# Attention with two heads per group of 32 rows, and the exponentials of ScalarE moved among its copies

## What is computed

```python
x = x + xattn(layernorm(x), ctx, ...)          # x, ctx: (16, 128, 256)
x = x + ffn(layernorm(x), ...)

def xattn(query, key, ...):                     # 16 heads of 16 numbers
    q, k, v = query @ Wq.T + bq, key @ Wk.T + bk, key @ Wv.T + bv
    att = q @ k.T / sqrt(16)                    # per head, 128 x 128
    att = where(pad_mask == 0, -1e9, att); att = where(subsq_mask == 0, -1e9, att)
    return softmax(att) @ v

def ffn(x):                                     # 12 experts, two per row, and a shared one
    logits = (x @ Wr + br) / 1.5
    top_val, top_idx = top_k(logits, 2); w = softmax(top_val)
    return shared(x) + sum(w_e * expert_e(x))   # each: GEGLU between two products
```

## Time and profile before

| | us |
|---|---|
| median of 3 runs | 661.57 (658.15 to 663.26) |
| span of the profiled execution | 661.7 |
| TensorE busy | 601.9 (91%) |
| VectorE busy | 460.1 (70%) |
| ScalarE busy | 302.4 (46%) |
| GpSimd busy | 348.7 (53%) |
| the chain that ended last, by engine | TensorE 68%, VectorE 11%, issue 7%, ScalarE 6% |

### The profile page before, as it was taken

One profiled execution on the slowest core, in us unless ns is written; L12 is line 12 of the kernel. 1 busy time (PEld: TensorE's weight loads), 2 busy tenths in 40 slices (PEclk: granted clock), 3 DMA queues, 4 the chain that ended last, 5 costly groups with the idle time before them and its releaser, 6 DMA issues.

```text
span 661.7 us, 14825 instructions
## 1 busy us (share of the span) xinstructions
PE 601.9 (91%) x4406; PEld 508.4 (77%) x4407; DVE 460.1 (70%) x1037; ACT 302.4 (46%) x677; POOL 348.7 (53%) x403
## 2 busy tenths in 40 slices
PE   7899999998887876989999999999999999997893
PEld 6677878887767765778878888788887888787792
DVE  7888888979865547766666667666776666653575
ACT  4467676655654223434444444344443444432331
POOL 3891100110294673998884893888893860006361
PEclk9999999989987977989999999999999999999798
DMA  8957465248404323345643544445633311003242
GB/s 278 333 212 258 153 223 206 88 183 295 176 28 172 122 94 86 144 156 196 223 145 109 184 170 137 139 136 209 219 137 127 125 42 40 24 18 99 77 137 79
DMA packets 47910, 98.95 MB, mean 150 GB/s; under 512 B 4736, under 2 KB 23808, under 8 KB 47872
## 3 DMA queue, kind: packets, MB, share of 16 engines
q1 hardware_dynamic: 36192, 50.40, 21.5%
q0 software_dynamic: 10976, 47.72, 21.5%
q10 hardware_dynamic: 704, 0.33, 0.2%
HBM read 57.15 MB, written 39.19 MB: 146 GB/s over the span
## 4 chain that ended last, share of the span: by engine, by line
PE 68%; DVE 11%; issue 7%; ACT 6%; another core or an unknown queue 4%; POOL 3%; DMA 1%; DVEq 0%; ACTq 0%; SPq 0%; POOLq 0%
PE ps_s L801 27%; PE ps_o L834 9%; PE ps_o L835 5%; PE ps_s L763 5%; PE ps_t L586 3%; PE ps_t L811 3%; PE ps_t L515 2%; PE ps_x L515 2%; ACT prob L1006 1%; DVE nmax L1351 1%; PE ps_s L811 1%; PE ps_o L596 1%; PE ps_x L822 1%; PE ps_s L574 1%
## 5 line engine op out<-in xcount | busy, mean ns | idle before, releaser
L801 PE MATMUL ps_s<-ring,xTh 128*128 (+1 forms) x516 | 152.2, 417 | 1.4 <-DVE xTl L1674 1.4
L1850 POOL TENSOR_TENSOR ring<-stage,ring 128x512 fp32r<-128x512 f32 x80 | 100.6, 1290 | 1.2
L801 PEld LDWEIGHTS ps_s<-ring,xTh 128*128 128x128 f32 x516 | 88.5, 189 | 16.1 <-DVE xTl L1674 1.6
L834 PE MATMUL ps_o<-ring,hTh 128*128 x258 | 97.0, 413 | 2.2 <-DVE hTl L1669 2.2
L1660 DVE TENSOR_TENSOR ag<-ps_s,up_bias 128x512 f32<-128x512 f32 x129 | 88.8, 689 | 12.4 <-PE ps_s L801 10.0
L801 PE MATMUL ps_s<-ring,xTl 128*128 (+1 forms) x258 | 80.6, 393 | 0.0
L835 PE MATMUL ps_o<-ring,hTl 128*128 x258 | 72.8, 282 | 0.0
L1836 POOL TENSOR_TENSOR ve<-mv,eps 128x2 f32<-128x2 f32 x16 | 3.9, 246 | 130.6 <-DVE mv L1390 117.2
L2036 POOL DMA_INDIRECT gath<-rows_out,idx_out x32 | 30.9, 967 | 77.2 <-DMA rows_out<-y_row 57.0
L1130 ACT ACTIVATE ps_s<-ag 128x256 f32<-128x256 f32 x129 | 50.2, 389 | 39.0 <-DVE ag L1660 37.9
L1665 DVE TENSOR_TENSOR ag<-ag,ps_s 128x256 f32<-128x256 f32 x129 | 54.3, 421 | 16.1 <-ACT ps_s L1130 0.5
(11 more groups left out here) (272 smaller groups left out, 1350.7 us busy)
## 6 DMA issues: line engine op xcount, KB each, us to landing
rows_in<-y_row SPq DMA_DIRECT2D x8, 3328.0 KB, 12.2
stage<-in_w POOLq DMA_DIRECT2D x12, 1536.0 KB
stage<-in_w POOLq DMA_DIRECT2D x12, 768.0 KB, 5.4
up_bias<-in_bias POOLq DMA_DIRECT2D x12, 768.0 KB, 4.6
xrow<-rows_in SPq DMA_DIRECT2D x43, 128.0 KB, 2.1
rows_out<-y_row SPq DMA_DIRECT2D x43, 128.0 KB, 1.7
cbuf<-in_ctx SPq DMA_DIRECT2D x8, 256.0 KB, 2.9
xn_all<-xn2p SPq DMA_DIRECT2D x8, 256.0 KB
```

The lines of the kernel that those rows point to most:

```text
L801: last = pe_.matmul(ps_s[:, i, :], x[:, c, :], weights(place, off + c * 2 * HR + i * 2 * D, 2 * D), start=n == 0, stop=n == 5)
L834: pe_.matmul(ps_o[:, :], hTh[i][:, c, :], weights(place, a, 2 * D), start=i == 0 and c == 0, stop=False)
L1850: last = pool.tensor_tensor(lo_ap[:, c:c + PIECE], src[:, c:c + PIECE], hi_ap[:, c:c + PIECE].bitcast(f32), ALU.subtract)
```

## The change

- **Two heads in a group of 32 rows.** The host orders the columns of wq and wk so that a group of 32 rows holds two heads. q and k are projected once, 256 columns in all: steps `k` and `q` of two parts take the place of `k0 k1 q0 q1`. So that a product over 32 rows gives one head's scores and not the sum of two, k is stored twice (`km_hi`, `km_lo`), once with the odd head's rows set to zero and once with the even head's; GpSimd writes these (`spread_keys`). `scores` has 24 products of 32 rows by 256 columns.
- **The context comes transposed from the host.** Step `cT` is gone; GpSimd splits the loaded context into high and low (`split_ctx`).
- **GpSimd applies both normalisations** (`normalise_x`, `normalise_rows`); VectorE's next statistics wait until it has.
- **SyncE's rounds**: load the context, then wait for the rows, save them, fill.
- **The shared expert's weights** are converted in slices inside the pairs 1 to 4, where the first loads of expert weights are issued too.
- **The order in the bodies.** A group of `values` follows each copy instead of four behind the fourth; ScalarE's exponentials stand between the second and third copies of the batch before (and between the third and the fourth of the next), ahead of its copies of k and q; `r` and `l` stand behind the last transposes.
- **Masks** come from one instruction, and the identity is scaled by the fill value.

The diff, cut:

```diff
@@ SyncE
+            sp.wait_ge(c_split, 1)
             load_ctx(1)
...
-            def pair(p, par, first, last):
-                if first:
-                    sp.wait_ge(xb_ready, index_of("cT", p, first, last) + 1)
-                    load_ctx(2)
-                else:
-                    save_xn2(p - 1)
-                sp.wait_ge(xb_ready, index_of("cT", p, first, last, first) + 1)
-                load_ctx(p + 3)
-                fill(p + 1)
+            def pair(p, first):
+
+                sp.wait_ge(c_split, p + 2)
+                load_ctx(p + 2)
+                if not first:
+                    save_xn2(p - 1)
+                fill(p + 1)
@@ TensorE, scores
-                for g in range(4):
-                    for k in (k_hi, k_lo):
+                for r in range(2):
+                    for n, (q, k) in enumerate(((q_hi, km_hi), (q_lo, km_hi), (q_hi, km_lo))):
                         for j in range(4):
...
+                            last = pe_.matmul(ps_s[:, j, r * 256:(r + 1) * 256].rearrange("p (a t) -> p a t", a=2),
+                                              q[par][rows, r, b * P:(b + 1) * P], k[par][rows, b, r, :, :],
+                                              start=False, stop=r == 1 and n == 2)
@@ TensorE, pair (not first)
                     prob_transposes(prev, 0)
+                    put("k", (0,))
                     prob_transposes(prev, 1)
+                    values(1, 1 - par, prev, (0,))
+                    put("k", (1,))
                     prob_transposes(prev, 2)
+                    values(1, 1 - par, prev, (1,))
+                    put("q", (0,))
                     prob_transposes(prev, 3)
+                    values(1, 1 - par, prev, (2,))
+                    put("q", (1,))
+                    values(1, 1 - par, prev, (3,))
+                    scores(p, par, 1)
+                    out_transposes(prev)
                     put("n")
...
+                prob_transposes(cur, 0)
+                put("v", (0,))
+                prob_transposes(cur, 1)
+                values(0, par, cur, (0,))
+                put("v", (1,))
+                prob_transposes(cur, 2)
+                values(0, par, cur, (1,))
+                put("xT", again=first)
+                prob_transposes(cur, 3)
+                values(0, par, cur, (2,))
+                put("r")
+                values(0, par, cur, (3,))
+                put("l")
+                out_transposes(cur)
+                next_scores()
@@ ScalarE, pair (not first)
                     prob_copy(prev, 0)
                     prob_copy(prev, 1)
-                    put("k0")
+                    exp(p * 4, 0)
                     prob_copy(prev, 2)
+                    sc.wait_ge(k_spread, p + 1)
+                    put("k")
                     prob_copy(prev, 3)
-                    put("k1")
                     out_copy(prev)
-                    exp(p * 4, 0)
                     exp(p * 4 + 1, 1)
-                    put("q0")
+                    put("q")
...
+                prob_copy(cur, 0)
+                prob_copy(cur, 1)
                 put("v")
+                prob_copy(cur, 2)
+                put("xT", first)
+                exp(p * 4 + 2, 2)
+                prob_copy(cur, 3)
+                put("r")
+                out_copy(cur)
                 exp(p * 4 + 3, 3)
@@ VectorE, ln1_stats and pair (not first)
+                if not (isinstance(pp, int) and pp == 0):
+                    ve.wait_ge(xn1_ready, pp)
...
                     softmax_add(p * 4, 0)
+                    softmax_shift(p * 4 + 1, 1, p * 2)
+                    put("k")
+                    if isinstance(p, int) and p == PAIRS - 3:
+                        choose(0, 0)
+                    elif not isinstance(p, int):
+                        ln1_stats(p + 3)
+                    softmax_max(p * 4 + 2, 2, p * 2 + 1)
+                    norm(p - 1, 1)
+                    put("q")
+                softmax_add(p * 4 + 2, 2)
                 if not first:
                     residual(p - 1, 1)
...
+                softmax_shift(p * 4 + 3, 3, p * 2 + 1)
+                put("xT", first)
                 norm(p, 0)
                 residual(p, 0)
@@ GpSimd
+            def split_ctx(q):
+
+                gp.wait_ge(ctx_in, 16 * (q + 1))
...
+                pool.tensor_scalar(hi[:, :, :], c_raw[:, :, :], 1.0, 0.0, ALU.mult, ALU.add).then_inc(c_hi, 1)
+                gp.wait_ge(c_hi, q + 1)
+                pool.tensor_tensor(lo[:, :, :], c_raw[:, :, :], hi[:, :, :].bitcast(f32), ALU.subtract).then_inc(c_split, 1)
...
+            for p in range(1, PAIRS - 1):
+                if p + 2 < PAIRS:
+                    split_ctx(p + 2)
+                    normalise_x(p + 2)
+                spread_keys(p + 1)
+                if p == 1:
+                    shared_up_hi()
+                if p == 2:
+                    shared_up_lo(0, W1S // 2)
+                if p == 3:
+                    shared_up_lo(W1S // 2, W1S)
+                if p == 4:
+                    shared_down()
+                    gp.wait_ge(converted, 1)
+                    load_raw1(0)
+                    load_raw2(0)
+                normalise_rows(p - 1)
```

More of the change, by code:

```diff
@@ L290, in build @@
     combined, stored = sem("combined"), sem("stored")
[L295 to L309, removed]
+    HI = ["k", "q", "xT"]
+    FIRST = ["k", "xT", "q", "v"]
+    HI_FIRST = [s for s in FIRST if s in HI]
+    first_bank = [ps_x[:, :], ps_s[:, 0, :], ps_s[:, 1, :], ps_t[:, 1, :]]
+    MASK_A = 2
     BATCHES = ((0, 8), (8, 12), (12, 16))
@@ L495, in transposes, with step @@
                 return last
-            def step(s, pp, idx, bank, first=False, parts=(0, 1)):
+            def step(s, pp, par, idx, bank, first=False, parts=(0, 1)):
                 if not first and 0 in parts:
@@ L595, in values @@
+            def values(b, par, batch, groups=(0, 1, 2, 3)):
+                for g in groups:
+                    pe.wait_ge(pt_copied, batch * 4 + g + 1)
+                    if g == 0 and not (isinstance(batch, int) and batch == 0):
+                        pe.wait_ge(normed, batch)
                     for j in range(4):
                         last = pe_.matmul(ps_o[32 * j:32 * j + VW, g * P:(g + 1) * P], v_sb[par][:, b, 4 * g + j, :],
-                                          probT[:, j, g, :], start=True, stop=True)
@@ L679, in put @@
                         return
-                    idx, bank = index_of(s, p, first, last, again), bank_of(s, p, par, first, last, again)
+                    idx, bank = index_of(s, p, first, last, again), bank_of(s, p, first, last, again)
                     if s == "n":
@@ L685, in put @@
                     else:
-                        step(s, p + (2 if s in AHEAD and (again or not first) else 1), idx, bank, parts=parts)
+                        step(s, p + (2 if s == "xT" and (again or not first) else 1), 1 - par, idx, bank, parts=parts)
                 def next_scores():
                     pe.wait_ge(xb_free, index_of("v", p, first, last) + 1)
+                    pe.wait_ge(k_spread, p + 2)
                     pe.wait_ge(masks_ready, 2)
@@ new lines, in shared_up_hi, with shared_up_lo @@
+            def shared_up_hi():
+                gp.wait_ge(shared_in, 32)
+                for c in range(0, W1S, PIECE):
+                    last = pool.tensor_scalar(ring[:, SH, c:c + PIECE], shared_w1[:, c:c + PIECE], 1.0, 0.0, ALU.mult, ALU.add)
+                last.then_inc(conv_hi, 1)
+            def shared_up_lo(c0, c1):
+                gp.wait_ge(conv_hi, 1)
+                for c in range(c0, c1, PIECE):
+                    pool.tensor_tensor(ring[:, SH, W1S + c:W1S + c + PIECE], shared_w1[:, c:c + PIECE],
+                                       ring[:, SH, c:c + PIECE].bitcast(f32), ALU.subtract)
```

498 lines of the change are left out of this document (213 added, 285 removed).

## The result

The changed kernel takes 704.16 us in the median of 4 runs (702.95 to 705.39), the kernel before 662.28 beside it: ratio 1.065 (95% interval 1.061 to 1.069). The profiled span is 701.1 us against 661.7; the mean granted clock of TensorE is 0.909 against 0.960. The prediction said 664 and at most 678.

A forecast was written before the change was run, and what follows sets the result against it. After the change a circle through SyncE's queue was to set the pace, 24.7 us a round; B(7) 0.6 us later plus 2 for the clock made 2.6 on 661.57, so 664 us, range 646 to 678.

The forecast's parts named there:

- The circle: Attention loop: rows ready, save, fill, context load behind the fill, GpSimd's work, next rows; 24.7 us a round.
- GpSimd's branch: GpSimd's in-order jobs between one pair's normalised rows and the next: 24.1 us, in pair 4 27.7.
- Rival 2: GpSimd's per-partition passes cost as much as two-input ones, so its branch decides: 677 us; chance 0.15.
- X(1): X(p) is when pair p's normalised rows are ready for the router; for pair 1 forecast at 58.3 us.
- B(1): Start of pair 1's body on TensorE, forecast at 43.0 us against 42.8 in the kernel before.
- VectorE's branch: VectorE's statistics wait for GpSimd's normalised x, then 6.0 us of its work; a round of 24.7 us.
- The chain of 19.8 us: Dependent steps across engines from one body's start to the next, if nothing else held: a gain of 2.7 us a pair.
- Rival 1: The circle through the sync queue is not closed, pairs 1 to 4 take 19.8 us: 643 us; chance 0.15.
- The router's tail: Steps from the normalised rows through the router to the next scores: 4.55 us, 8.0 at half clock.
- Rival 3: TensorE's clock stays lower beyond the tail in every pair, 2 us on each of five: 672 to 674; chance 0.15.
- Costs at nothing: Items priced at zero, among them ScalarE's q and k copies behind the exponential, covered by the wait for the circle.
- B(7): Start of pair 7's body on TensorE: 184.9 against 184.3 us, its shift passing to the end nearly one for one.

The follow-up runs named there:

- e1: The changed kernel with SyncE loading the context of one pair further on, ahead of its wait for the normalised rows; ratio 1.041 to the kernel before.
- e18: e7 with GpSimd's four key-spreading passes written in four instruction forms, two without masking; a single run, 650 us, the kernel before beside it 631.
- e3: The changed kernel with GpSimd's key-spreading passes multiplied by the constant 1.0 instead of the column of ones and zeros, without masking; ratio 1.067 to the kernel before.
- e16: e10 with GpSimd normalising x of the third pair first, then spreading the second pair's keys, then splitting the third context; ratio 0.999 to the kernel before.
- e17: e16 with ScalarE's third exponentials of a body behind its fourth copy of probabilities and its output copy; ratio 0.985, 652.0 against 661.4 us for the kernel before.
- e10: e5 with the router's tail reordered: last values product, output transposes and next masks ahead of the rows' transposes, logits last; ratio 1.007 to the kernel before.
- e5: e1 with GpSimd's slice of the shared weights behind its normalisation of the rows, not ahead of it; ratio 1.025 to the kernel before.
- e11: The changed kernel with ScalarE's first exponentials of a body behind its copy of the output again; ratio 1.068 to the kernel before.
- e14: e10 with ScalarE's first exponentials of a body behind its copy of the output again; ratio 1.007 to the kernel before.
- e8: The kernel before with the context load (three pairs on) behind the fill, not ahead of it; ratio 1.000 to the kernel before.
- e7: e1 with the spread keys in a flat layout, so a spreading pass handles 512 neighbouring elements; ratio 1.043 to the kernel before.
- e6: e5 with the rows' normalisation, not that of x, done by VectorE again; ratio 1.044 to the kernel before.
- e12: e6 with GpSimd waiting for the normalised rows ahead of its slice of the shared weights; ratio 1.033 to the kernel before.

## Why the prediction was wrong, point by point

- **The circle: right.** It closes as described, by the load behind the fill; the loads of pairs 4 to 7 land 10.7 to 11.9 us after issue where 12 to 13 was named as the sign, and GpSimd's waits of 12.9 to 14.0 answer the 13.0 of the sum. e1 shows that it is the circle and not the place in the queue alone.
- **The term that failed: GpSimd's passes.** The sum for GpSimd's branch was 24.1 us; measured from 69.13 to 100.76 it is 31.6. Term by term (predicted, measured): wait 13.0, 14.0; split 2.1, 2.0; root and x 1.75, 3.5; spreading 2.8, 6.2; slice 2.6, 2.5; root and rows 1.85, 3.5. The three terms with GpSimd's new passes are 6.8 of the 7.5 us. A spreading pass was bounded by 0.61 and 1.25 and took 1.55; a normalising pass by 0.31 and 0.63 and took 1.22. Both lie above the upper bound: rows of other forms did not bound a form that the trace didn't hold. That these 6.8 us count in full is read from the round shown above, in which GpSimd has no gap behind the context; no run has the circle with cheaper passes. The rule that single-input passes are cheap was applied to a form for which e18 shows the opposite. (The Trainium skill, "GPSIMD Engine Reference", section "Engine selection", calls single-input work roughly line-rate; the 0.62 us of one form agrees, the 1.50 of the other does not.)
- **Rival 2 came nearest:** GpSimd's branch decides, and by the prediction's own terms it does so above 0.85 us a spreading pass. Its price, 677, was too low for the same reason, and its cause was not the one named: with a constant in place of the per-partition operand a pass still took 1.50 us (e3). Against the forecast each of pairs 2 to 5 is 6 to 7 us longer, X(1) 10.8, pair 6 6.7.
- **B(1) at 43.0: wrong, 51.2.** The spreading of pair 1 was taken as covered by the arrival of the context at 32.8. At 6.2 us it ends at 36.1 and moves the split and the normalisation; x is ready at 42.5, not 36.8. Again the same term, through GpSimd's order; e16 shows that the order alone hides most of it.
- **VectorE's branch (24.7): there, but not deciding.** Its statistics waited for GpSimd's x (2.87 us before 88.76), while GpSimd's own branch was 7 us longer.
- **The chain of 19.8 us: about right, and not reached.** With both circles gone and another order of the tail e17 has 20.4. TensorE's work was less well reckoned: 20.0 us a pair before and 16.3 after, where the traces have 21.9 busy before and 19.3 after, both at full clock (e10), so the gain was 2.6 us and not 3.7. And the list of what stands ahead of the rows on GpSimd (spreading and slice, waiting for the k copy) was left out of the chain: e1 and e5 show the second circle that this makes. Rival 1 (643, a ratio of 0.97) would not have come true even with the first circle open: e1 is at 1.041.
- **The router's tail, 4.55: measured 8.0** in pairs 1 to 4, the value that the text gave for half clock. There it is hidden in the circle, as said: GpSimd waits for the context meanwhile. Behind X(5) and X(6) it is not, and took 7.6 and 7.3, together 5.8 us above two times 4.55, where the sum put 2 out of 0 to 7.
- **Rival 3, the clock.** It stayed low beyond the tail (0.77 over the whole of pair 2), but within the circle GpSimd sets the pace. Where TensorE's own work is in the chain the clock does cost: 3.6 us a pair in e5 against e10.
- **Costs at nothing.** The exponentials ahead of the k copy: right (e11, e14). Those ahead of the fourth copy were not priced; they cost 1.3 us of waiting a pair where nothing covers them (e10, e16), and 0.3 remain without them (e17).
- **The shift of B(7) passes to the end: nearly.** 45.3 us at B(7), 39.4 at the end. The rest of the program took 5.9 us less than before, at the same granted clock of 0.95; why was not tried.

## What to carry to other kernels

Before work is given to an engine that runs its program in order, write down what stands ahead of each of its outputs and what each of those jobs waits for: here one job waiting for a transfer, a copy or a statistic held up rows that had nothing to do with it, and each circle opened showed the next. A load that is needed in such a round is issued a round before its use; behind the big write it may then stand (e1, e8). And a new form of an instruction is priced by a run of that form; if none is to be had, the nearest row is no upper bound: here the passes took 2.5 and 4 times what the nearest row gave.

## What the hardware showed

- **GpSimd's pass with a scalar depends on the form:** 128 x 512 with a multiplication alone 1.50 us (1.56 with a column), with a multiplication and an addition of 0.0 it is 0.62 (0.69 with a column), in the same layout (e18); `km_hi` alone was measured in both forms, 1.57 and 0.69 with a column (e7, e18).
- **VectorE beside GpSimd:** a 128 x 256 normalising pass took 1.25 to 1.35 us beside GpSimd's two-input passes and 0.41 alone (e6, e12).
- **TensorE's clock followed its waits:** over a whole pair the granted clock was 0.83 with one wait of 2.6 us in it, and 1.00 without it; the same products kept TensorE busy 22.8 and 19.3 us (e5, e10).
- **A 256 KB load right behind a 3.3 MB write on the same queue** landed after 10.7 to 11.9 us, and the same kind of load ahead of it after 3.0 (the changed kernel and the kernel before).
